# The layer norms' last steps on ScalarE, their reciprocal deviations as a power on GpSimd, and the router's top two in three slots

## What is computed

```python
def _layernorm(x, axis=-1, eps=1e-05):
    m = jnp.mean(x, axis=axis, keepdims=True)
    v = jnp.var(x, axis=axis, keepdims=True)
    return (x - m) / jnp.sqrt(v + eps)
...
    # _L0_ffn_ref, E = 8 experts, K = 2
    logits = jnp.einsum('tc,ec->te', x_flat, router_w)
    probs = jax.nn.softmax(logits, axis=-1)
    top_w, top_idx = jax.lax.top_k(probs, K)
    top_w = top_w / (jnp.sum(top_w, axis=-1, keepdims=True) + 1e-09)
    h = jax.nn.relu(jnp.einsum('tc,efc->tef', x_flat, w1) + b1[None])
    y = jnp.einsum('tef,ecf->tec', h, w2) + b2[None]
    out = jnp.einsum('tkc,tk->tc', jnp.take_along_axis(y, top_idx[:, :, None], axis=1), top_w)
...
    x = x + 0.5 * _L0_ffn_ref(_layernorm(x, axis=-1), ...)
    x = x + _L0_attn_ref(_layernorm(x, axis=-1), ...)
    x = x + 0.5 * _L0_ffn_ref(_layernorm(x, axis=-1), ...)
```

## Time and profile before

| | |
|---|---|
| median of 3 runs | 518.18 us (518.05 to 520.53) |
| the profiled execution | 518.44 us, of which its span is 516.60 |
| slot 0 begins | 11.10 us after the span's start |
| a slot of TensorE with nothing laid over it | 1.55 us |
| slot 97, where unit 1's scans begin, begins on TensorE | 198.14 us after the span's start |
| VectorE's idle time ahead of its combine in slot 139, where unit 2's scans begin | 1.09 us |
| busy: TensorE, VectorE, ScalarE, GpSimd | 486.4, 373.3, 287.3, 222.2 us |

### The profile page before, as it was taken

The page is one execution under the profiler, slowest core; times in us unless marked ns, Lnnn a source line. Parts: engine busy times, 40 slices in busy tenths (PEclk is TensorE's granted clock), DMA queues, the critical chain, the costliest instruction groups (busy, mean ns, idle before and its releaser), DMA issues.

```text
span 516.6 us, 5885 instructions
## 1 busy us (share of the span) xinstructions
PE 486.4 (94%) x1782; PEld 288.8 (56%) x1782; DVE 373.3 (72%) x704; ACT 287.3 (56%) x447; POOL 222.2 (43%) x228
## 2 busy tenths in 40 slices
PE   7999999999999999999988968999996999999996
PEld 3566675565455446554644634555562545677774
DVE  3555188759958699995977799857869984666443
ACT  2766587654346565344557423357752435587873
POOL 0034320649951245884024358811517882113222
PEclk9999999999999999999999999999999999999999
DMA  7191111074310017710003625111054411003100
GB/s 226 55 369 47 41 42 41 3 223 162 105 41 1 1 41 186 243 62 1 1 0 128 200 82 158 48 62 41 0 145 144 153 71 41 0 1 124 63 0 20
DMA packets 20575, 43.52 MB, mean 84 GB/s; under 512 B 3776, under 2 KB 3904, under 8 KB 20544
## 3 DMA queue, kind: packets, MB, share of 16 engines
q1 hardware_dynamic: 14208, 31.61, 18.8%
q10 hardware_dynamic: 6336, 11.54, 7.1%
HBM read 39.86 MB, written 3.28 MB: 83 GB/s over the span
## 4 chain that ended last, share of the span: by engine, by line
PE 54%; issue 18%; POOL 13%; DVE 12%; ACT 2%; POOLq 0%; DVEq 0%; ACTq 0%
PE Y L316 17%; PE U L295 7%; PE U L297 7%; PE U L296 7%; POOL xT L809 5%; POOL qs L825 5%; PE Y L311 2%; PE Y L313 2%; PE Y L312 2%; DVE hid_lo L680 2%; PE A L385 2%; DVE pool_a L733 2%; POOL carry L822 2%; POOL pool_a L831 1%; DVE xnt L615 1%
## 5 line engine op out<-in xcount | busy, mean ns | idle before, releaser
L501 ACT ACTIVATE hid<-U,small 128x512 f32<-128x512 f32 x188 | 128.7, 687 | 157.9 <-PE U L297 145.2
L316 PE MATMUL Y<-hid,w 128*128 128x512 f32 x376 | 191.8, 591 | 0.0
L809 POOL TENSOR_TENSOR xT<-xT,gy 128x512 f32<-128x512 f32 x64 | 87.1, 1360 | 213.2 <-DVE gy L689 213.1
L295 PE MATMUL U<-xhi,w1lo 128*128 128x512 f32 x256 | 168.2, 657 | 7.7 <-ACT hid L501 6.6
L297 PE MATMUL U<-xhi,w1hi 128*128 128x512 f32 x256 | 101.1, 395 | 0.0
L296 PE MATMUL U<-xlo,w1hi 128*128 128x512 f32 x256 | 100.3, 392 | 0.0
L825 POOL TENSOR_TENSOR qs<-q,pool_a 128x512 f32<-128x512 f32 x64 | 82.3, 1285 | 21.8 <-DVE pool_a L716 21.8
L295 PEld LDWEIGHTS U<-xhi,w1lo 128*128 128x128 f32 x256 | 48.3, 189 | 74.7 <-issue 56.5
L316 PEld LDWEIGHTS Y<-hid,w 128*128 128x128 f32 x376 | 70.8, 188 | 16.1
L680 DVE TENSOR_TENSOR hid_lo<-hid,hid_hi 128x512 fp32r<-128x512 f32 x68 | 52.6, 780 | 26.8 <-ACT hid_hi L499 26.5
L296 PEld LDWEIGHTS U<-xlo,w1hi 128*128 128x128 f32 x256 | 48.6, 190 | 38.7 <-issue 36.9
(11 more groups left out here) (122 smaller groups left out, 469.0 us busy)
## 6 DMA issues: line engine op xcount, KB each, us to landing
G<-gate_dram SPq DMA_DIRECT2D x32, 512.0 KB, 4.0
vb<-v_dram ACTq DMA_DIRECT2D x44, 256.0 KB, 3.3
vb<-v_dram SPq DMA_DIRECT2D x20, 256.0 KB, 4.3
pool_a<-wexp_dram SPq DMA_DIRECT2D x8, 256.0 KB, 7.0
w<-wexp_dram SPq DMA_DIRECT2D x8, 256.0 KB, 7.1
v_dram<-v SPq DMA_DIRECT2D x8, 256.0 KB, 2.2
xT<-xT_dram SPq DMA_DIRECT2D x4, 256.0 KB, 7.9
out_dram<-xT SPq DMA_DIRECT2D x4, 256.0 KB, 2.8
```

The lines of the kernel that those rows point to most:

```text
L295: mm(dst, w1lo[:, e, f, :], xhi[:, k % NB, :], start=True, stop=False)
L316: mm(dst, w2[:, g % E, f, :], hid[:, n % HS, :], start=first, stop=final).then_inc(down, 1)
L501: act.activation(hid[:, n % HS, :], U[n % 2][:, :], ACT.Relu, bias=bias).then_inc(h_f, 1)
L809: pool.tensor_tensor(xT[:, h, b, :], xT[:, h, b, :], gy[:, g % 2, :], ALU.add).then_inc(acc, 1)
```

## The change

- ScalarE's root is gone. VectorE adds epsilon to the variances (new L614), GpSimd raises the sum to the power -0.5 at `T_DEV` (new `deviation`, L818, four numbers a partition), and VectorE makes minus mean times rstd at `T_NRM` (`scales`, L619).
- ScalarE then normalises with four activations at `T_NRM`, Identity with a scale and a bias for each partition (`normalise`, new L478), in place of VectorE's reciprocal and its four passes.
- Steps 1 to 5 of the router stand in three slots, as 1 and 2, 3 and 4, and 5. The factor 0.5 goes into step 4, so that step 5 has one instruction less. The gates go to DRAM two slots earlier.
- At the start ScalarE splits w1 before it normalises.

```diff
-    return max(4 * (k * E + (c + 1) * EQ - GS) + 4, PREP[k] + T_RT + 5 if k else 0)
+    return max(4 * (k * E + (c + 1) * EQ - GS) + 4, PREP[k] + T_RT + 3 if k else 0)
...
-                    if n == PREP[k] + T_RT + 5:
+                    if n == PREP[k] + T_RT + 3:
                         gates_to_rows(k)
...
-            def deviation(ln):
-                act.wait_ge(ln_var, ln + 1)
-                v = slice(ln % 2 * 4, ln % 2 * 4 + 4)
-                act.activation(std[:, v], mv[:, v, 1], ACT.Sqrt, bias=epsc[:, 0:1]).then_inc(ln_std, 1)
+            def normalise(ln, bank):
+                act.wait_ge(ln_rst, ln + 1)
+                for t in range(4):
+                    at = ln % 2 * 4 + t
+                    last = act.activation(xnt[:, at, :], bank[:, t * P:(t + 1) * P], ACT.Identity,
+                                          bias=shift[:, at:at + 1], scale=rstd[:, at:at + 1])
+                last.then_inc(ln_nrm, 1)
...
-            act.activation(table[:, :], epsc[:, :], ACT.Sqrt)
-            deviation(0)
             split_w1(0)
+            normalise(0, A[0])
             ffn_hi(0, A[0])
...
-                last.then_inc(ln_var, 1)
-
-            def normalise(ln, bank):
-                dve.wait_ge(ln_std, ln + 1)
-                t0 = ln % 2 * 4
-                link(dve.reciprocal(rstd[:, t0:t0 + 4], std[:, t0:t0 + 4]))
-                for t in range(4):
-                    last = dve.tensor_scalar(xnt[:, t0 + t, :], bank[:, t * P:(t + 1) * P],
-                                             mv[:, t0 + t, 0:1], rstd[:, t0 + t:t0 + t + 1], ALU.subtract, ALU.mult)
-                last.then_inc(ln_nrm, 1)
+                last.then_inc(ln_mv, 1)
+                dve.wait_ge(ln_mv, ln + 1)
+                dve.tensor_scalar(std[:, t0:t0 + 4], mv[:, t0:t0 + 4, 1], EPS, None, ALU.add).then_inc(ln_var, 1)
+
+            def scales(ln):
+                dve.wait_ge(ln_rsd, ln + 1)
+                v = slice(ln % 2 * 4, ln % 2 * 4 + 4)
+                dve.scalar_tensor_tensor(out=shift[:, v], in0=mv[:, v, 0], scalar=-1.0, in1=rstd[:, v],
+                                         op0=ALU.mult, op1=ALU.mult).then_inc(ln_rst, 1)
...
-                    link(dve.tensor_tensor(m(3), m(7), m(2), ALU.mult))
+                    link(dve.scalar_tensor_tensor(out=flat(m(3)), in0=flat(m(7)), scalar=0.5, in1=flat(m(2)),
+                                                  op0=ALU.mult, op1=ALU.mult))
...
-                    link(dve.tensor_scalar(r(5), r(7), 0.5, None, ALU.mult))
-                    link(dve.tensor_tensor(gate[:, b].rearrange("p e t -> p t e"), m(3), bc(r(5)), ALU.mult))
+                    link(dve.tensor_tensor(gate[:, b].rearrange("p e t -> p t e"), m(3), bc(r(7)), ALU.mult))
...
-                if T_RT <= t < T_RT + 5:
-                    route(k, t - T_RT + 1)
+                if T_RT <= t < T_RT + 3:
+                    for step in ((1, 2), (3, 4), (5,))[t - T_RT]:
+                        route(k, step)
...
+            def deviation(ln):
+                v = slice(ln % 2 * 4, ln % 2 * 4 + 4)
+                pool.wait_ge(ln_var, ln + 1)
+                pool.tensor_tensor(rstd[:, v], std[:, v], half[:, 0:1].to_broadcast([P, 4]), ALU.pow).then_inc(ln_rsd, 1)
```

More of the change, by code:

```diff
@@ L126, in program @@
         std = sb("std", [P, 8])
-        table = sb("table", [P, 1])
+        half = sb("half", [P, 1])
         rstd = sb("rstd", [P, 8])
+        shift = sb("shift", [P, 8])
         epsc = sb("epsc", [P, 1])
@@ L178, in program @@
         w1hi_s, w1lo_s, rw_r, setup, out_done = sem("w1hi_s"), sem("w1lo_s"), sem("rw_r"), sem("setup"), sem("out_done")
-        ln_src, ln_var, ln_std, ln_nrm, ln_T = (sem(n) for n in ("ln_src", "ln_var", "ln_std", "ln_nrm", "ln_T"))
+        ln_src, ln_mv, ln_var, ln_rsd, ln_rst, ln_nrm, ln_T = (sem(n) for n in ("ln_src", "ln_mv", "ln_var", "ln_rsd", "ln_rst", "ln_nrm", "ln_T"))
         xn_hi, xn_lo, xa_rdy = sem("xn_hi"), sem("xn_lo"), sem("xa_rdy")
         lg, lg_sub, p_exp, g_row, warm = sem("logits"), sem("logits_sub"), sem("p_exp"), sem("gate_rows_r"), sem("warm")
+        half_s = sem("half_s")
         up, h_f, h_lo, down = sem("up"), sem("h_f"), sem("h_lo"), sem("down")
@@ L508, in prepare @@
             def prepare(k, t):
-                if t == T_DEV:
-                    deviation(LN_FFN[k])
+                if t == T_NRM:
+                    normalise(LN_FFN[k], A[3])
                 if t == T_CHN:
@@ L522, in attend @@
                 h, b = home(i)
-                if t == T_DEV:
-                    deviation(LN_ATT[i])
+                if t == T_NRM:
+                    normalise(LN_ATT[i], A[0])
                 m = scan_at(t - 1)
@@ L695, in prepare @@
                 if t == T_NRM:
-                    normalise(LN_FFN[k], A[3])
+                    scales(LN_FFN[k])
                 if t == T_LO:
@@ L723, in attend @@
                 if t == T_NRM:
-                    normalise(LN_ATT[i], A[0])
+                    scales(LN_ATT[i])
                 if t == T_XM:
@@ L777, in _ @@
             dve.tensor_tensor(rwh[:, 1, :], w(W_RT, E), rwh[:, 0, :], ALU.subtract).then_inc(rw_r, 1)
-            normalise(0, A[0])
+            scales(0)
             split_w1(0)
@@ L856, in _ @@
             due = {combine_slot(g): g for g in range(BLOCKS * E)}
+            pool.memset(half[:, :], -0.5).then_inc(half_s, 1)
             pool.memset(hid[:, HS - 1, :], 0.0).then_inc(warm, 1)
+            pool.wait_ge(half_s, 1)
+            deviation(0)
             for n in range(ALL):
+                for k in range(1, BLOCKS):
+                    if n - PREP[k] == T_DEV:
+                        deviation(LN_FFN[k])
+                for i in range(UNITS):
+                    if n - UNIT[i] == T_DEV:
+                        deviation(LN_ATT[i])
                 if n in due:
```

## The result

The changed kernel took 521.05 us (median of 20 runs, 519.21 to 523.75), the kernel before 518.93 us (20 runs beside it, 517.08 to 520.66). The ratio is 1.0037 with a 95% interval from 1.0024 to 1.0049: about 2 us slower, where 3 us less had been forecast. The profiled execution took 520.48 us with a span of 518.5 us, against 518.44 and 516.60.

What follows compares the result with a forecast made beforehand. TensorE, busy 486.4 of 516.60 us, was taken as the bound, so only its waits counted. Nine places summed to -3.0 us, giving 515.2 us against 518.18, with a range of 512.5 to 518.

Steps and rivals of the forecast that it cites:

- Unit 1's values: Slot 103: values queue behind block 3's gates and 1 MB of loads, first product 5.3 us late; +4.1 us (0.3 to 6.0).
- Slot 44: Block 2's exponential: a 1.28 us table load goes, ScalarE gets two normalises just ahead; -0.4 us (0 to -0.8).
- third rival: ScalarE late, waiting for VectorE's L619 with `relu` behind; 0.4 us for each later layer norm, 4.4 in all: 519.5; chance 0.14.
- slots 84 to 86: Slot 85: TensorE's 1.6 us wait for L764 goes with VectorE's two normalises, `relu` comes some 0.7 late; -0.9 us.
- The start: Up to slot 4: wait of `relu(1)` goes with its table load, first layer norm gets longer; -0.5 us (-0.8 to +0.3).
- the sign named for it: GpSimd's power in the new profile: expected below 1 us, priced at 0.5; over 2 us would make the prediction wrong.
- Small steps: All slots outside the named places: a slot in which TensorE does not wait stays as it is; 0 us.
- The scans: First scans of units 2 and 3: router steps no longer stand between the products; -3.0 and -1.1 us.
- Slots 126 to 134: Slots 128 to 133: step 2 ahead of L767 costs 0.9, moved step 5 and normalise end L331's 2.2 wait; -1.3 us.
- slot 174: Forecast as slot 173: a ScalarE table load of 1.28 us goes; -0.4 us.
- slots 92 to 94: Slots 89 to 93: router steps 3 and 4 ahead of L733's last products cost 0.9, later 0.4 is gained; +0.5 us.
- The rival in which the scans' gain does not come: Scans' reduction has another wait, for GpSimd, right behind: 4.1 us back, 519, or 517 with unit 1's loss halved; chance 0.10.

Runs made afterwards that it cites:

- q1: e4 with the gates written to DRAM two slots early but the loads that read them back left late; 513.25 us, ratio 0.9896 to the kernel before.
- e3: Kernel before with only the router's part of the change: three slots, gates two slots earlier, layer norms as before; 518.44 us, ratio 0.999.
- e4: Kernel before with only the router in three slots, gates going to DRAM as late as before, layer norms as before; 513.24 us, ratio 0.9895.
- n3: e1 with the normalising passes back on VectorE, the power still on GpSimd; 513.86 us, ratio 0.9912 to the kernel before.
- n6: e1 with ScalarE's root and VectorE's reciprocal in place of the power, ScalarE still normalising; 518.12 us, ratio 0.9984 to the kernel before.
- n11: e1 with minus mean times rstd made by GpSimd behind its power, from VectorE's negated mean; 511.73 us, ratio 0.9845 to the kernel before.
- e1: The changed kernel with the gates going to DRAM as late as before the change; 515.62 us, ratio 0.9938 to the kernel before.
- n8: e1 with each GpSimd power made twice, the first into a buffer nobody reads; 518.2 us, ratio 0.9993 to the kernel before.
- e2: Kernel before with only the layer norms' part of the change, router in five slots and gates late; 520.53 us, ratio 1.0038.

## Why the prediction was wrong

In the traces, by which the forecast was made, it missed by 4.9 us: +1.85 for -3.0 (by the medians 5.1). Both traces have the full clock up to slot 253, so none of the miss is the clock. Six of its nine places came within 0.5 us, and they erred by 1.4 us in all towards too little gain. The other three and what was forecast as nothing erred by 6.2 us towards too much gain.

**Unit 1's values, mis-sized: +4.1 forecast, +5.84 measured.** The mechanism was right, and q1 shows that it is the 1 MB. Everything in the changed trace lies 1.35 us later there by what the places before have cost, so 1.35 is to be taken off for a comparison. The issue of v, 194.10, becomes 192.75 (192.4 forecast), and the first product, 203.88, becomes 202.53 (202.2 forecast). So it came 5.7 us late and not 5.3, with the same 9.8 us from the issue to the product. Then VectorE's lead of 1.3 us should have covered its part. In e3 it did: there the first product came 202.53 - 0.48 - 196.86 = 5.2 us late, and TensorE lost 3.94. In the changed kernel the lead was used up by the second product. VectorE in e3, products 0 and 1, and then both in the changed kernel with GpSimd between them:

```profile
202.53 0.70 DVE L709 TENSOR_TENSOR A<-vb,kk 128x512 f32<-128x512 f32 x1 [5.28 <-DMA vb<-v_dram]
204.50 0.68 DVE L709 TENSOR_TENSOR A<-vb,kk 128x512 f32<-128x512 f32 x1
```

```profile
206.14 1.28 POOL L834 TENSOR_TENSOR qs<-q,pool_a 128x512 f32<-128x512 f32 x1
206.15 1.83 DVE L712 TENSOR_TENSOR A<-vb,kk 128x512 f32<-128x512 f32 x1 [0.21 <-DMA vb<-v_dram]
```

The second values were 0.21 us late, GpSimd's product of the first state began 0.01 us ahead, and VectorE's product took 1.83 us instead of 0.68. With the first product's 0.4 us that is 0.21 + 1.15 + 0.4 = 1.8, against 5.84 - 4.1 = 1.7 to be explained. Also, "all of it as waits ahead of the reduction" was wrong: two waits of TensorE are for `relu` (1.56 and 1.36 us), behind `fetch`, and one of 1.91 is the reduction's. The whole lies within the bounds given (0.3 to 6.0).

**Slot 44, wrong in sign: -0.4 forecast, +1.70 measured.** The sum there held ScalarE's work only: one table load less, 1.28 us, against two normalises more, 3.2. These terms by themselves speak for a loss, and no row gave the -0.4. It also took no account of what ScalarE waits for ahead of them. The forecast said that the power's result "is wanted one slot later, so anything up to about 1.5 us is hidden". That left out what follows the power: a turn in VectorE's order, a product, and a further hand-over to ScalarE, with the `relu` behind. This is the third rival's mechanism ("it waits for VectorE's L619 with the next `relu` behind it"), to which 0.14 was given. The rival spread 0.4 us over eleven layer norms, 4.4 in all. Removing the hand-over gave 3.9 us, but in the trace 2.7 of it are two places, slots 38 to 45 (+1.70 became -0.06) and slots 84 to 86. "ScalarE's 56%" was held against it, and that was the wrong argument. ScalarE's share of busy time says nothing on whether it stands waiting in its own order. What should have been read is VectorE's order in slots 36 and 39: what stands ahead of L619 there, and what GpSimd does at that time.

**The start, -0.5 forecast, +0.14 measured.** The power took 1.02 us there instead of 0.5, which explains most of it; the sign named for it, below 1 us, did not come. The forecast's wait of `relu(1)` went as it was said, 1.08 us at slot 3 in place of 1.20, and slot 0 came 1.22 us later instead of 0.65. The +0.14 is within the bounds that the power was given there (-0.8 to +0.3). With the 0.4 us by which the start moves from one execution to the next, one profile settles no more than that.

**Small steps, 0 forecast, +0.41 in slots 5 to 37 and +1.35 elsewhere.** In slots 5 to 37 it is spread evenly, some 13 ns a slot. It is a term that the forecast put at nothing with the words that a slot in which TensorE does not wait stays as it is. e4, without any part of the layer norms' change, has 0.00 and 0.07 instead. n3, in which ScalarE normalises nothing, and n6, which has no power, both have 0.41 in slots 5 to 37, and n11 has 0.18. So it belongs to that part, but neither to the power nor to ScalarE's activations alone. Its cause is open.

**Right.** L478 at 461 ns (0.48 forecast), nine table loads, the wait for the normalise at slot 133 down from 2.2 to 0.45 us (none was forecast), and unit 2's first product at 299.92 with its fourth at 305.88, 5.96 us apart (some 6 forecast). The scans gave 3.20 and 1.53 us for 3.0 and 1.1. Slots 126 to 134 gave the 1.31 that was forecast, slot 174 gave 0.48 for 0.4, slots 84 to 86 1.31 for 0.9, and slots 92 to 94 cost 0.24 for 0.5. All of that was cancelled by the two places above. The rival in which the scans' gain does not come is refuted by e4.

The rule of the Trainium skill, "ScalarE: Activation LUTs", section "Rules for kernel authors", that additions and multiplications belong on VectorE, was weighed in the prediction and turned down. By e1 and n3 it holds here, by 1.8 us. By n11, in which ScalarE does the same activations and the kernel is 2.1 us faster than n3, it does not. Between e1 and n11 the activations stay as long as they were (461 and 464 ns), and the wait ahead of them falls from 11.6 to 1.6 us.

## What to carry to other kernels

When a small step moves to another engine, write out the whole chain of hand-overs that it now has (here VectorE, GpSimd, VectorE, ScalarE) and read for each link what stands ahead of it in that engine's order. The step's own duration is the smaller part, and a busy share of 56% does not protect an engine that waits in order. When a transfer may start earlier, look at what it overtakes in its queue: here 1 MB that nobody wanted yet took 5 us from 512 KB that VectorE was waiting for, and moving only the small write early (q1) cost nothing. Read the granted clock of a stretch before a difference there is put down to an edit: here 3.4 us of half clock made 1.6 us of difference at slots 129 and 130 between kernels in which TensorE does the same there. And take a change of several parts apart by place: this one was a gain of 5.4 us, a loss of 5.2 and a loss of 2.4, and one of the losses was turned into a gain by a single product made elsewhere.

## What the runs showed of the hardware

- GpSimd's power of 128x4 elements takes 1.01 or 1.02 us in eight cases and 1.39 in four (1.14 on average in the changed kernel), nearly as much as its product of 128x512 (1.30), while its product of 128x4 takes 0.20 us (n11). At this size the price is the function's. The second of two in a row takes 1.01 us (n8).
- A small VectorE product of two operands in SBUF is held until GpSimd's running addition ends: 0.16 us alone, up to 1.25 beside a running GpSimd instruction, and in six of six such cases its end lies 0.01 to 0.02 us behind that one's. The Trainium skill, "SBUF — State Buffer", section "SBUF: two separate sides", says that VectorE and GpSimd share a pair of SBUF ports as an exclusive lock: of a VectorE instruction with two SBUF inputs and a GpSimd instruction that reads SBUF, the one that starts first has the pair until it ends. The trace agrees. For four numbers the price is that of the neighbour. The 128x512 product L712 is longer beside GpSimd's product too, 1.83 us against 0.68, and ends 0.56 us behind it, in the place where unit 1 lost its lead.
- Two loads of 512 KB ahead in SyncE's queue lengthened the round of a 512 KB write from issue to the first reload from 2.7 to 6.6 us.
- Nine table loads of 1.28 us were taken out, 11.5 us in all. Their return together with the root (n6) cost TensorE 0.7 us at slots 38 to 45 and 1.15 at slots 135 to 143, and by the medians 2.5 us against e1. The next activation begins 0.01 to 0.04 us after a load's end (the kernel before).
- In five of the fourteen traces TensorE's granted clock fell to 0.50 for one stretch of 3.4 us, each time with, or within 1.4 us behind, the end of a wait of 2.2 to 2.5 us: at 10.6 us in e1 (busy 1.40 of the 3.6 us before), at 261.2 in n11 (1.25 of 3.2), at 10.4 in e2, at 265.8 in n8 and at 267.8 in e3. It cost 0.86 us at the start and 1.6 at slots 129 and 130. The changed kernel's trace has waits of 2.87 and 2.49 us at the same places and no such stretch.
